# A one-core transformer block: token types as one row spread by TensorE, other order of loads, halves and fillers in the opening

## The reference

```
def expert_mask(tt):
    vm = jnp.zeros(tt.shape, dtype=bool)
    vm = vm.at[:, :-1].set((tt[:, :-1] == 1) & (tt[:, 1:] == 1))
    return vm

def rms_norm(x, w):
    xf = x.astype(jnp.float32)
    var = jnp.mean(xf * xf, axis=-1, keepdims=True)
    return (w * (xf * jax.lax.rsqrt(var + EPS))).astype(x.dtype)
```

## Time and profile before

| | us |
|---|---|
| runs | 1474.73, 1470.37, 1474.76; median 1474.73 |
| profiled execution | 1476.38 |
| its span, first to last instruction | 1474.6 |

### The profile page before, as it was taken

One profiled execution on the slowest core, in us unless ns is written; L12 is line 12 of the kernel. 1 busy time (PEld: TensorE's weight loads), 2 busy tenths in 40 slices (PEclk: granted clock), 3 DMA queues, 4 the chain that ended last, 5 costly groups with the idle time before them and its releaser, 6 DMA issues.

```text
span 1474.6 us, 20618 instructions
## 1 busy us (share of the span) xinstructions
PE 1403.8 (95%) x7850; PEld 740.6 (50%) x7851; DVE 906.7 (61%) x1429; ACT 581.3 (39%) x880; POOL 553.7 (38%) x385
## 2 busy tenths in 40 slices
PE   6979899999999989998998999999999999999998
PEld 3446555555555544444654455555344355555344
DVE  6896766666667616421226788887433778888540
ACT  1264366666666652001442344444122434444121
POOL 2630388888888891000001144452000144453000
PEclk9999999999999999999999999999999999999999
DMA  7000623232323204004842011110042001110000
GB/s 274 0 2 20 165 70 90 67 92 71 88 66 92 52 13 191 0 0 174 335 124 71 0 39 39 40 39 1 0 122 70 1 27 39 39 39 13 1 0 25
DMA packets 45019, 95.62 MB, mean 65 GB/s; under 512 B 6860, under 2 KB 28892, under 8 KB 44908
## 3 DMA queue, kind: packets, MB, share of 16 engines
q1 hardware_dynamic: 44912, 94.21, 21.0%
HBM read 72.04 MB, written 0.97 MB: 50 GB/s over the span
## 4 chain that ended last, share of the span: by engine, by line
PE 84%; DVE 8%; POOL 3%; issue 2%; ACT 2%; DMA 0%; SPq 0%; DVEq 0%; ACTq 0%; POOLq 0%
PE psum L1658 23%; PE psum L2175 10%; PE psum L1899 5%; PE psum L1875 5%; PE psum L1849 4%; PE psum L2107 4%; PE psum L1832 3%; PE psum L2138 3%; PE psum L1818 3%; POOL XN L708 3%; PE psum L2165 2%; PE psum L2170 2%; DVE WA L1341 2%; PE psum L2167 2%; PE psum L2166 2%
## 5 line engine op out<-in xcount | busy, mean ns | idle before, releaser
L1341 DVE TENSOR_REDUCE WA<-psum 112x2 f32<-112x1000 f32 x192 | 229.8, 1200 | 89.9 <-PE psum L1849 89.9
L708 POOL TENSOR_TENSOR XN<-XN,WBZ 125x896 f32<-125x896 f32 x128 | 266.5, 2082 | 16.8 <-POOL XN L708 0.9
L1052 ACT ACTIVATE WA<-psum,y_bias 125x448 f32<-125x448 f32 x192 | 118.6, 633 | 208.9 <-PE psum L2170 190.4
L933 ACT ACTIVATE WBZ<-psum 125x896 f32<-125x896 f32 x192 | 175.5, 915 | 43.9 <-PE psum L1875 33.3
L2175 PE MATMUL psum<-WA,ctxN 125*128 125x448 f32 x384 | 180.9, 554 | 0.8 <-ACT WA L1052 0.7
L740 POOL TENSOR_TENSOR XN<-const,y_max 112x896 bf16<-112x896 f32 x32 | 75.2, 2350 | 246.2 <-DVE y_max L1557 189.2
L731 POOL TENSOR_SCALAR ctxT<-ctxT 128x375 f32<-128x375 f32 x32 | 56.2, 1756 | 250.9 <-ACT std L806 248.4
L1557 DVE CUSTOM_DVE_ANT_0 XA<-psum,WA 112x375 bf16<-112x375 f32 x240 | 125.3, 541 | 37.6 <-PE psum L2138 36.6
L1875 PE MATMUL psum<-R 100*125 100x224 f16 x768 | 110.7, 266 | 0.0
L1570 DVE RECIPROCAL WBZ<-WBZ 128x224 f32<-128x224 f32 x68 | 105.1, 1546 | 0.1
L1875 PEld LDWEIGHTS psum<-R 100*125 100x125 f16 x768 | 78.9, 136 | 28.3 <-issue 25.0
(11 more groups left out here) (255 smaller groups left out, 2337.9 us busy)
## 6 DMA issues: line engine op xcount, KB each, us to landing
R<-WA SPq DMA_DIRECT2D x192, 93.8 KB, 2.2
WA<-in_ctxT SPq DMA_DIRECT2D x14, 750.0 KB, 4.3
ctxT<-in_ctxT SPq DMA_DIRECT2D x11, 750.0 KB, 4.2
ctxN<-in_ctx SPq DMA_DIRECT2D x32, 192.0 KB, 2.5
ctxT<-in_ctxT SPq DMA_DIRECT2D x32, 187.5 KB, 2.4
R<-in_ctx SPq DMA_DIRECT2D x7, 768.0 KB, 7.3
R<-in_ctxT SPq DMA_DIRECT2D x7, 750.0 KB, 7.2
WA<-in_ctx SPq DMA_DIRECT2D x6, 768.0 KB, 6.4
```

The lines of the kernel that those rows point to most:

```text
L708: nc.gpsimd.tensor_tensor(z_sum[b % 2][0:TK, :], first[0:TK, :], z_p[t % 4][0:TK, :], ALU.add)\
L933: nc.scalar.activation(z_p[t % 4][0:TK, :].rearrange("p (k n) -> p k n", k=2), psum[0:TK, s:s + 2, 0:2 * GC], ACT.Exp, scale=float(CHD0) * ...
L1052: nc.scalar.activation(y_pT[t][0:TK, g * HALF:(g + 1) * HALF], bank[2 + u % 3][0:TK, 0:HALF], ACT.Exp, bias=y_bias[0:TK, bass.ds(b * NT + ...
L1341: V.tensor_reduce(z_mx[0:PR, r:r + 3:2, c], psum[0:PR, lo:lo + 2, 0:PC], AX_X, ALU.max)\
```

## The change

In five parts, all in the opening:

- The token types are loaded as one row on one partition with a semaphore of their own. DVE makes the expert mask as a row (`vm_row`) on one partition; PE spreads it to 128 partitions by a product with a row of ones, each half into a bank (4 and 5); DVE reads the first half's mask from the bank for the split, then copies both to `vm`.
- X is loaded directly behind the constants; positions and the two masks come behind X.
- DVE weighs and splits the first half first, inverts its deviation, evacuates two projections, and only then weighs and splits the second half. The second half's inversion stands between the first half's evacuations 4 and 5.
- PE computes eight filler products (`warm`, 224 columns, their results unused, into bank 0): four ahead of the spreading products and four behind them, in front of the variance.
- POOL sets its ones first.

```diff
@@ block.sync
-            load(ints[:, :], a["token_types"], "masks_in")
-            load(posi[0:S, :], a["positions"], "masks_in")
-            load(masku[0:B, :].bitcast(I32), a["mask"], "masks_in")
-            load(masktu[0:TK, :].bitcast(I32), a["maskT"], "masks_in")
+            load(ints[0:1, :], a["token_types"], "types_in")
             load(const[:, :], a["const"], "const_in")
             load(vec[:, :, :], a["vectors"], "const_in")
             load(gates[:, :], a["gates"], "const_in")
             load(X[:, :, :], a["xT"].rearrange("(k p) t -> p k t", p=P), "x_in")
+            load(posi[0:S, :], a["positions"], "masks_in")
+            load(masku[0:B, :].bitcast(I32), a["mask"], "masks_in")
+            load(masktu[0:TK, :].bitcast(I32), a["maskT"], "masks_in")
@@ block.gpsimd
+            nc.gpsimd.memset(ones[:, :], 1.0)
+            nc.gpsimd.memset(minusb[:, :], -1.0).then_inc(sem("ones_ready"), 1)
             nc.gpsimd.memset(small[:, :], 0.0)
             nc.gpsimd.memset(eps6[:, :], 1e-6)
             nc.gpsimd.memset(eps5[:, :], 1e-5).then_inc(sem("small_clear"), 1)
-            nc.gpsimd.memset(ones[:, :], 1.0)
-            nc.gpsimd.memset(minusb[:, :], -1.0).then_inc(sem("ones_ready"), 1)
@@ block.vector
+            dve.wait_ge(sem("types_in"), 16)
+            is1 = R[0:1, 0:T]
+            then(V.tensor_scalar(is1, ints[0:1, :], 1.0, None, ALU.is_equal))
...
+            V.memset(vmv[:, :, S - 1:S], 0.0)
+            V.tensor_tensor(vmv[:, :, 0:S - 1], is1v[:, :, 0:S - 1], is1v[:, :, 1:S], ALU.mult)\
+                .then_inc(sem("vm_row"), 1)
+            dve.wait_ge(sem("const_in"), 48)
             dve.wait_ge(sem("small_clear"), 1)
-            dve.wait_ge(sem("masks_in"), 64)
-            dve.wait_ge(sem("const_in"), 48)
...
             dve.wait_ge(sem("x_in"), 16)
-            weigh("n1", "L0_xattn_ln_in_w")
-            for h in range(2):
-                dve.wait_ge(sem("n1_ready"), h + 1)
-                by_expert("experts1", h)
-
-            inverse_roots("n1")
+            weigh_half("n1", "L0_xattn_ln_in_w", 0)
+            dve.wait_ge(sem("n1_ready"), 1)
+            dve.wait_ge(sem("vm_spread"), 1)
+            by_expert("experts1", 0, bank[4][:, 0:HT])
+            for h in range(2):
+                last = V.tensor_copy(vm[:, half(h)], bank[4 + h][:, 0:HT])
+            then(last)
+            inverse_half("n1", 0)
...
             for m in range(2):
                 leave(0, m)
+            weigh_half("n1", "L0_xattn_ln_in_w", 1)
+            dve.wait_ge(sem("n1_ready"), 2)
+            by_expert("experts1", 1)
+            dve.wait_ge(sem("masks_in"), 48)
             then(V.tensor_copy(masktf[0:TK, :], masktu[0:TK, :]))
...
             for m in range(4, 3 * KD):
                 leave(0, m)
+                if m == 4:
+                    inverse_half("n1", 1)
@@ block.tensor
+            def warm(bk, n):
+
+                for _ in range(n):
+                    pe.matmul(bank[bk][:, 0:GC], mean, const[:, 0:GC], start=True, stop=True)
+
+            warm(0, 4)
+            pe.wait_ge(sem("ones_ready"), 1)
+            pe.wait_ge(sem("vm_row"), 1)
+            for h in range(2):
+                mm = pe.matmul(bank[4 + h][:, 0:HT], ones[0:1, :], vm_row[:, half(h)], start=True, stop=True)
+            mm.then_inc(sem("vm_spread"), 1)
+            warm(0, 4)
             variance("n1")
```

More of the change, by code:

```diff
@@ L354, in build @@
         ints = R[:, 12800:12800 + T].bitcast(I32)
+        vm_row = R[0:1, T:2 * T]
         posi = R[:, 13700:13700 + S].bitcast(I32)
@@ L1116, in inc_empty, with weigh_half, inverse_half @@
                 ins.then_inc(sem("emptied_dve"), 1)
-            dve.wait_ge(sem("small_clear"), 1)
-            dve.wait_ge(sem("masks_in"), 64)
-            dve.wait_ge(sem("const_in"), 48)
[L1122 to L1126, removed]
+            dve.wait_ge(sem("types_in"), 16)
+            is1 = R[0:1, 0:T]
+            then(V.tensor_scalar(is1, ints[0:1, :], 1.0, None, ALU.is_equal))
+            is1v, vmv = is1.rearrange("p (b s) -> p b s", b=B), vm_row.rearrange("p (b s) -> p b s", b=B)
+            V.memset(vmv[:, :, S - 1:S], 0.0)
+            V.tensor_tensor(vmv[:, :, 0:S - 1], is1v[:, :, 0:S - 1], is1v[:, :, 1:S], ALU.mult)\
+                .then_inc(sem("vm_row"), 1)
+            dve.wait_ge(sem("const_in"), 48)
+            dve.wait_ge(sem("small_clear"), 1)
+            def weigh_half(tag, w, h):
+                for k in range(KD):
+                    last = V.tensor_scalar(XN[:, k, half(h)], X[:, k, half(h)], vector(w, k), None, ALU.mult)
+                last.then_inc(sem(tag + "_ready"), 1)
             def weigh(tag, w):
                 for h in range(2):
-                    for k in range(KD):
-                        last = V.tensor_scalar(XN[:, k, half(h)], X[:, k, half(h)], vector(w, k), None, ALU.mult)
-                    last.then_inc(sem(tag + "_ready"), 1)
+                    weigh_half(tag, w, h)
+            def inverse_half(tag, h):
+                dve.wait_ge(sem(tag + "_std"), h + 1)
+                then(V.reciprocal(std[:, half(h)], std[:, half(h)]))
             def inverse_roots(tag):
                 for h in range(2):
-                    dve.wait_ge(sem(tag + "_std"), h + 1)
-                    then(V.reciprocal(std[:, half(h)], std[:, half(h)]))
+                    inverse_half(tag, h)
             def normalise(tag, src, dst, w):
@@ L1148, in normalise, with by_expert @@
                     last.then_inc(sem(tag + "_ready"), 1)
-            def by_expert(tag, h):
+            def by_expert(tag, h, which=None):
+                which = vm[:, half(h)] if which is None else which
                 for k in range(KD):
-                    last = V.tensor_tensor(XA[:, k, half(h)], XN[:, k, half(h)], vm[:, half(h)], ALU.mult)
+                    last = V.tensor_tensor(XA[:, k, half(h)], XN[:, k, half(h)], which, ALU.mult)
                 then(last)
@@ L1901, in attended @@
                 mm.then_inc(sem("z_pv"), 1)
-            def warm(bk, n):
-                for _ in range(n):
-                    pe.matmul(bank[bk][:, 0:GC], mean, const[:, 0:GC], start=True, stop=True)
             pe.wait_ge(sem("z_clear"), 1)
@@ L2278, in arrange @@
     arrays = {
[L2279 removed]
+        "token_types": c(np.asarray(mask_BxS_ik0).reshape(1, T)),
         "positions": c(np.broadcast_to(np.asarray(pos_1xS).reshape(1, S), (S, S))),
```

1 line of the change is left out of this document (removed).

## The result

| | before | after |
|---|---|---|
| median | 1474.7 (1469.85 to 1477.42, 20 runs) | 1478.26 (1475.51 to 1499.78, 20 runs) |
| ratio to before, 95% interval | | 1.0047 (1.0028 to 1.0065) |
| profiled execution | 1476.38 | 1483.58 |
| its span | 1474.6 | 1481.8 |
| setup products start | 41.93 | 46.65 |

A forecast was written before the change was run, and what follows sets the result against it. The setup was taken to wait for DVE's index arithmetic: projections from 14.6 plus 27.4 give 42.0 against 41.93, the 2.6 us won on PE being spent on DVE. Shifted +0.1 us, the median 1474.7 becomes 1474.8; range 1470.8 to 1478.0.

The forecast's parts named there:

- s: Start of PE's first product, once the constants have landed: 4.6 us (4.4 to 5.3).
- Rival (c): Opening loads: constants land no earlier than now (6.4), setup at 43.9, +2.0 us, 1476.7; chance 0.05.
- x: PE's time at 1.2 GHz from its first product in the opening: taken as 5.0 us, from 3.4, 5.0 and 6.05.
- fewer rows cost no less: PE's two spreading products of 448 columns: one row costs as much as more, together 1.50 us.
- The row on 64 rows: Profile row cited for the spreading products' price: a product with 64 rows takes 587 ns.
- Ps: Start of PE's projections, behind the variance: 14.6 us (13.6 to 15.9) instead of 17.24.
- of 1.0 us each: Two DVE operations on the types in the opening, ending by 6, before the fourth filler does.
- Ps + 27.4: When DVE lets the setup start: 27.4 us behind the projections' start, now 24.7; setup at 42.0 against 41.93.
- The forecast wait of 3.3 us: PE's idle time ahead of the setup products, waiting for DVE: 3.3 us instead of 0.64.
- Rival (b): PE's clock falls in the new wait before the setup, costing 1.7 to 3.0 us: 1476.5 to 1477.8; chance 0.25.
- 3.54 us without a product up to 690.61: Argument against a clock fall before the setup: this earlier gap left the clock at 1.00, and the new wait is shorter.
- A rigid shift: Everything behind the setup keeps order and sizes, so it moves as one by +0.1 us (-0.9 to +1.4).

The follow-up runs named there:

- e1: after with POOL's long memset started only when DVE has the row of types done; median 1480.4, ratio 1.0058.
- e3: after with the second half's reciprocal between evacuations 1 and 2 instead of between the fifth and sixth; median 1480.4, ratio 1.0014.
- r4: after run once more, unedited; median 1479.94, ratio 1.0033, four of 12 runs at 1492 to 1496.
- s1: before with only the second half's reciprocal moved to the change's place, between the fifth and sixth evacuation; median 1485.04, ratio 1.0072.
- s2: before with eight fillers (224 columns, 128 rows) directly ahead of the variance; median 1472.18, ratio 1.0002.
- r1: s2 with three fillers once in the memory cross-attention; median 1473.13, ratio 0.9986.
- r3: Control: before with only the three fillers in the memory cross-attention; median 1475.32, ratio 1.0003.
- e2: e1 with the types spread by products of 128 rows, the rows other than the mask's being zero; ratio 1.0125.
- e6: e2 with the second half weighed and split before the first reciprocal, and the second reciprocal between evacuations 1 and 2; median 1474.35, ratio 1.0020.
- e8: e6 with three fillers once in the memory cross-attention; median 1473.86, ratio 0.9997.
- r2: after with three fillers once in the memory cross-attention; median 1474.92, ratio 1.0015.
- e7: after without its eight fillers; median 1484.43, ratio 1.0064.

## Why the prediction was wrong, step by step

- **s, the loads: right.** First product at 4.70 (forecast 4.6). X landed 6.3 us after its issue at 2.54, at 8.8 (forecast 8.3, and 7.0 to 9.2), the weights at 13.3 (13.2). Rival (c) is out.
- **x, the time at the lower clock: this step failed.** It was 12.25 us in the profiled execution, outside the 3.4 to 6.05 of the earlier trace rows; e1, e3 and r4 give 11.7, 11.7 and 11.8. Where only products of 128 rows stand in front, it is 2.9 to 5.2 (before, s1, s2, r1, r3, e2, e6, e8), and 3.85 in r2, where the clock rose before the one-row products; so the value taken from before was right for such products. The prediction let products of one row count for the clock like any others. The sentence "fewer rows cost no less" was right too, of time. The row on 64 rows behind it says nothing of what few rows do to the clock, and that wasn't asked. The Trainium skill, "TensorE: Matmul & The Clock Gate", section "Step-by-step: what each phase is for", says of the weight load that the number of rows doesn't matter to its time. Of time the traces agree (at the upper clock a weight load of the spreading products took 0.18 us with one row in r2, 0.19 with 128 in e2). To the clock the rows did matter: it rose 11.7 us after the first product in e1, 4.6 in e6 and 4.5 in e8.
- **Ps: 19.07 instead of 14.6, the sum of four terms.** s +0.10; the ten products took 9.74 us instead of 7.0, +2.74 (of it 2.06 because the clock stayed down for the whole block, and 0.68 because prices at the lower clock are above twice those at the upper); PE's gap +0.74; the variance +0.89. Together 4.47.
- **DVE's two operations "of 1.0 us each": half wrong, for 0.7 us.** One took 5.11, beside POOL's memset. The row that priced them, 1.00 us from 6.55, stood beside that memset too, and says when the memset lets go rather than what the comparison takes:

```profile
2.46 4.61 POOL L645 MEMSET R<- 128x5408 f32 x1
```

The memset ends at 7.07 in before as in after, and the comparison at 7.55 and 7.53.

- **DVE up to the setup, Ps + 27.4: right.** After 27.58, e1, e2, e7, r2 and r4 27.57 or 27.58; with the reciprocal early, e3 25.07 and e6 24.85. The gain is indeed spent on DVE, and s1 shows that one move accounts for it. The forecast wait of 3.3 us was 3.36.
- **Rival (b), chance 0.25: it came.** The clock fell at or behind the setup in all seven profiles with the wait of 3.36 us (after, e1, e2, e7, s1, r2, r4) and in none of the seven with 0.64 to 0.85 (before, e3, e6, e8, s2, r1, r3). The argument against it, 3.54 us without a product up to 690.61, came from another stage; its price, 1.63 us in after, was close to the low end of 1.7 to 3.0 (s1 2.5). In r2, where the opening came nearly as forecast and the fall lasted 6.8 us, the profiled execution took 1475.0, within the range: (b) by itself doesn't carry the time out of it.
- **"A rigid shift" behind the setup: this failed.** Order and sizes there are unchanged, but not what the clock does: nine of the 32 runs of after are at 1491 to 1500, and each profile of a high run (r4 of after, and e3, e7 and s1 of the others) loses 15 to 17 us in the cross-attention. No view of before's trace shows such a stretch, and the prediction had no case for it. This, with x, carries the result out of the range: with x the setup came at 46.65 instead of 42.0, and without the five high runs the median would be 1477.5, still inside.

What stays open is why before never falls there. Lateness alone isn't it: at 166 us r4 is 3.0 us late against before and has the stretch, e1 is 3.1 late and hasn't it, e3 is 0.4 early and has it. Which detail of the stage's timing decides it, no run here shows, nor whether the few rows or columns of its products do. In the runs with the three fillers it wasn't seen; fewer fillers, or others, weren't tried.

## What to carry to other kernels

Ask of an added matmul how many rows it uses as well as how long it takes: a spread by a one-row product is short, but at a kernel's start, with the clock still down, it kept it down, and the same product over 128 rows, 127 of them zero, didn't. Before moving work off one engine, count what waits on the next: here a reciprocal of 2.9 us, put ahead of the work that PE waits for, ate the gain and made a wait in which the clock fell. And where single runs of a kernel lie far above the others, judge an edit by the distribution of its runs and their mean clock: here three fillers in one stage went with the end of a group of runs 15 us up, which was more than any edit of the opening was worth.

## What the runs showed of the hardware

- PE at 1.2 GHz without a break while busy: 11.4 us in e1 with one-row products among the first; and, busy for 40.46 of 40.85 us, in r4, in a stage where most products have 32 rows or 32 columns of weights. Three fillers of 128 rows in one gap of the latter stage (1.30 us) stand in the 35 runs of a changed opening that have no time over 1486.
- A one-partition comparison on DVE took 5.11 us (after) and 5.15 (r2) when it started at 2.42 and 2.40, just ahead of POOL's memset at 2.46; 0.82 to 0.87 when it started at 2.13 to 2.18 (e3, e7, r4), and then the memset took 5.09 us instead of 4.61; and 0.70 with the memset moved away (e1). Over 128 partitions, in before, s2, r1 and r3, it started at 6.52 to 6.92 and ended at 7.54 or 7.55 each time; in s1 it started at 6.99, just ahead of POOL's next memset (7.01 to 7.53), and ended at 8.02. The Trainium skill, "SBUF — State Buffer", section "SBUF: two separate sides", describes a port pair that POOL and DVE, in operations of certain kinds, take as an exclusive lock, the one that starts first holding it for its whole instruction; whether the comparison is of such a kind, no run here shows. That one is held up by the other agrees (the memset ends at 7.07, the comparison at 7.53 to 7.55), and so does who wins in e3, e7 and r4. In after, r2 and s1 it doesn't: there the comparison had started 0.02 to 0.06 us before the memset, and was the one held up.
